# Routing stage with the residual add on VectorE, another order of instructions and another way into the experts; last pass with the hidden blocks transposed through memory and VectorE

## The reference

```python
x = x + tanh(g_xattn) * ssm(ctx, layernorm(x))          # the scan; its result is the "gated" addend
xn = layernorm(x)
scores = sigmoid(xn @ gate_w.T); sc = scores + gate_bias
# 4 groups of 8 experts: keep the 2 groups with the largest sum of their top two, then the top 4 experts
idx = top_k(where(group kept, sc, 0), 4); w = scores[idx] / sum(scores[idx]) * 2.0
# each expert takes its first 256 tokens in order, later ones are dropped
routed = sum_k w_k * (silu(xn @ w1[e]) * (xn @ w3[e])) @ w2[e]
shared = (silu(xn @ shared_gate) * (xn @ shared_up)) @ shared_down      # hidden width 1024
out = x + tanh(g_ffn) * (routed + shared)
```

## Time and profile before

| what | value |
|---|---|
| median of 3 runs | 4038.11 us (4036.43 to 4038.69) |
| the profiled execution, its own time | 4033.5 us |
| its span in the trace | 4031.7 us |
| busy: PE, DVE, ACT, POOL | 3681.9, 3111.3, 2114.9, 2008.3 us |
| routing stage / experts / last pass | about 1725 to 2386 / 2386 to 3479 / 3479 to 4032 us |

### The profile page before, as it was taken

The page is one execution under the profiler, slowest core; times in us unless marked ns, Lnnn a source line. Parts: engine busy times, 40 slices in busy tenths (PEclk is TensorE's granted clock), DMA queues, the critical chain, the costliest instruction groups (busy, mean ns, idle before and its releaser), DMA issues. The chain is left out here.

```text
span 4031.7 us, 58882 instructions
## 1 busy us (share of the span) xinstructions
PE 3681.9 (91%) x20528; PEld 3051.6 (76%) x20528; DVE 3111.3 (77%) x3712; ACT 2114.9 (52%) x2610; POOL 2008.3 (50%) x1201
## 2 busy tenths in 40 slices
PE   8898498888888888869999979999999999999999
PEld 3444388888878888758887868888888888788887
DVE  7899899999999999978888866666666666455555
ACT  3678699889989989821111134444444444200000
POOL 0233199999999999923333333333333333122222
PEclk9999599999999999979999989999999999999999
DMA  7677853653553553377766667777777777677543
GB/s 235 242 280 277 288 166 101 167 163 111 151 174 116 147 168 120 99 235 218 225 215 211 225 209 255 249 251 250 248 253 248 250 252 250 224 281 257 196 161 120
DMA packets 374393, 835.44 MB, mean 207 GB/s; under 512 B 96656, under 2 KB 155792, under 8 KB 364880
## 3 DMA queue, kind: packets, MB, share of 16 engines
q1 hardware_dynamic: 339264, 765.97, 56.3%
q0 software_dynamic: 34816, 67.24, 5.8%
q10 hardware_dynamic: 144, 0.00, 0.0%
HBM read 619.21 MB, written 245.27 MB: 214 GB/s over the span
## 5 line engine op out<-in xcount | busy, mean ns | idle before, releaser
L1125 POOL TENSOR_TENSOR h<-h,c 128x1024 f32<-128x1024 f32 x512 | 1206.4, 2417 | 24.4 <-DVE h L1108 21.5
L1108 DVE TENSOR_TENSOR_SCAN h<-da,dbu 128x1024 f32<-128x1024 f32 x512 | 1135.2, 2273 | 47.1 <-ACT dbu L1070 27.9
L1078 ACT ACTIVATE da<-dl,ad 128x1024 f32<-128x1024 f32 x512 | 584.2, 1141 | 100.3 <-DVE h L1108 88.9
L1157 PE MATMUL psy<-ident,h 128*128 128x128 f32 x4096 | 562.1, 281 | 81.6 <-POOL h L1125 60.6
L1903 POOL DMA_INDIRECT xg<-scratch_xn,ids x256 | 328.9, 1285 | 597.9 <-DVE xT_place L2190 520.1
L1070 ACT ACTIVATE dbu<-psb 128x512 f32<-128x512 f32 x1020 | 548.0, 589 | 30.7 <-PE psb L1147 27.9
L1157 PEld LDWEIGHTS psy<-ident,h 128*128 128x128 f32 x4096 | 444.9, 142 | 129.6 <-POOL h L1125 91.2
L2195 DVE TENSOR_TENSOR wsp<-arena,wsp 128x2048 fp32r<-128x2048 f32 x146 | 329.7, 2287 | 91.9 <-ACT wsp L2140 91.8
L1147 PE MATMUL psb<-m,du_taps 128*128 128x128 f32 x2048 | 294.6, 291 | 43.6 <-ACT dbu L1070 35.1
L1147 PEld LDWEIGHTS psb<-m,du_taps 128*128 128x128 f32 x2048 | 259.3, 193 | 79.5 <-ACT dbu L1070 73.0
L1451 POOL DMA_INDIRECT scratch_tab<-tok_s,si_s x128 | 132.1, 1032 | 358.8 <-DVE si_s L1819 327.4
(11 more groups left out here) (244 smaller groups left out, 8667.2 us busy)
## 6 DMA issues: line engine op xcount, KB each, us to landing
arena<-in_w SPq DMA_DIRECT2D x192, 1024.0 KB, 7.0
du_taps<-scratch_duT SPq DMA_DIRECT2D x496, 128.0 KB, 2.9
c<-scratch_c SPq DMA_DIRECT2D x64, 512.0 KB, 13.0
scratch_xT<-xT_s SPq DMA_DIRECT2D x32, 1024.0 KB
scratch_ob<-ob SPq DMA_DIRECT2D x64, 512.0 KB, 2.6
xT_place<-scratch_xT SPq DMA_DIRECT2D x32, 1024.0 KB, 4.9
scratch_duT<-duT SPq DMA_DIRECT2D x52, 512.0 KB, 4.0
xz<-in_x SPq DMA_DIRECT2D x32, 512.0 KB, 5.5
```

Of the source, the lines that this page charges most:

```text
L1078: act.activation(da[k % 2][:, :], dl[:, i % 2, :], ACT.Exp, scale=ad[:, i % 2, n:n + 1]).then_inc(s_da, 1)
L1108: dve.tensor_tensor_scan(h[:, k % HR, :], da[k % 2][:, :], dbu[:, (k // GN) % 2, k % GN, :], 0.0, ALU.mult, ALU.add).then_inc(s_scan, 1)
L1125: pool.tensor_tensor(h[:, k % HR, :], h[:, k % HR, :], c[:, n, :], ALU.mult).then_inc(s_hc, 1)
L1157: mm = pe.matmul(psy[:, t, :], h[:, k % HR, t * P:(t + 1) * P], ident[:], is_transpose=True, start=(n == 0 and t % 4 == 0), stop=(n == NST ...
```

## The change

In the **routing stage** the residual add goes from GpSimd to VectorE (in `norm`), the normalised tile is written by ScalarE (`normalise`, as scale * x + bias with bias = -mean * scale) and no longer by VectorE (`permuted` is gone), the Newton step has two instructions and no longer three, and VectorE's order is another: norm first, then queue, h_rest, x_blocks, choose, x_rest, multiply.

On the **way to the experts** the w2 matrix of expert 0 is loaded at the end of the routing stage, the rest of w3 is made after the first tile of rows (`first_up_rest`), w1 of expert 1 is loaded only after that, and VectorE multiplies expert 0's first hidden tile earlier.

In the **last pass** TensorE's `h_transpose` is gone. ScalarE stores the hidden tile to memory (`store_hidden`), waits for that, reads it back in four quarters (`load_hidden`), VectorE transposes 32x32 blocks (`h_blocks`), and head and rest are made from it. `finish` stands behind `h_rest`, and in it the read of `psO` comes first.

The core of the diff (renamings, semaphores and the like left out):

```diff
     for _ in range(NEWTON):
         st.then(dve.scalar_tensor_tensor(out=tmp[:, 1:2], in0=y, scalar=y, in1=tmp[:, 0:1], op0=ALU.mult, op1=ALU.mult))
-        st.then(dve.tensor_scalar(tmp[:, 1:2], tmp[:, 1:2], -0.5, 1.5, ALU.mult, ALU.add))
-        st.then(dve.tensor_tensor(y, y, tmp[:, 1:2], ALU.mult))
+        st.then(dve.scalar_tensor_tensor(out=y, in0=tmp[:, 1:2], scalar=1.5, in1=y, op0=ALU.add, op1=ALU.mult))
...
             if route:
                 first_ids()
+                for half in range(2):
+
+                    sp.wait_ge(s_wlo, 6 + half + 1)
+                    sp.dma_start(raw[:, 0, halves[half]].rearrange("p (k f) -> p k f", k=KF // 2),
+                                 io["w2"][0].rearrange("(h k p) f -> h p k f", h=2, p=P)[half]).then_inc(early["w2"][half], 16)
...
-                        if not (isinstance(t, int) and t >= TT - 3):
-                            add_x(j + 1 + par, 1 - par)
...
-                    if not route and not first:
-                        h_transpose(t - 1)
...
+            def normalise(t, j, par):
+
+                act.wait_ge(s_sc, t + 1)
+                after(act, s_xnst[par], j * 16)
+                act.activation(xn[:, par, :].rearrange("p (q j c) -> p j q c", q=NQ, c=QB),
+                               xt[:, par, :].rearrange("p (j q c) -> p j q c", q=NQ, c=QB), ACT.Identity, bias=rstd[:, 1:2],
+                               scale=rstd[:, 0:1]).then_inc(s_xn, 1)
...
+                    if not route and not first:
+                        load_hidden(t - 1)
                     if not first:
                         h_head(t - 1)
+                    if route and not first and not (isinstance(t, int) and t >= TT - 2):
+                        normalise(t + 2, j + 1, par)
 
                     act.wait_ge(s_g, t + 1)
-                    after(act, s_htr, t)
-                    act.activation(sg[:], psG[:], ACT.Silu).then_inc(s_sg, 1)
+                    if route:
+                        after(act, s_htr, t)
+                    act.activation(gated_hidden, gate_product, ACT.Silu).then_inc(s_sg, 1)
+                    if not route:
+                        store_hidden(t)
...
+            def store_hidden(t):
+
+                act.wait_ge(s_h, t + 1)
+                act.dma_start(dr["h"][t], sg[:]).then_inc(s_hst, 16)
+
+            def load_hidden(t):
+
+                act.wait_ge(s_hst, t * 16 + 16)
+                after(act, s_hlo, t)
+                for q in range(NQ):
+                    act.dma_start(hq[q * QB:(q + 1) * QB, :].rearrange("p (g c) -> p g c", g=NQ),
+                                  dr["h"][t][:, q * P:(q + 1) * P].rearrange("(g p) c -> p g c", g=NQ)).then_inc(s_hq, 16)
...
+            def h_blocks(t):
+
+                dve.wait_ge(s_hq, (t + 1) * 16 * NQ)
+                dve.transpose(hq[:], hq[:]).then_inc(s_htr, 1)
...
             def finish(t, j, par):
...
                 dve.wait_ge(s_acl[par], j * 32 + 32)
+                if not last:
+                    half()
...
-                dve.wait_ge(s_d, t + 1)
-                dve.scalar_tensor_tensor(out=x1t[:, par, :], in0=psO[:], scalar=gate[:, 0:1], in1=x1t[:, par, :],
-                                         op0=ALU.mult, op1=ALU.add).then_inc(s_half, 1)
+                if last:
+                    half()
...
                 after(dve, s_xn, t)
...
+                dve.tensor_tensor(xt[:, par, :], xt[:, par, :], xin[:, par, :], ALU.add).then_inc(s_add, 1)
...
-                    if route and not first:
-                        queue(t - 1, j - (par == 0), 1 - par)
                     if route and first:
                         norm(1, 0, 1)
                     elif route and not (isinstance(t, int) and t >= TT - 2):
                         norm(t + 2, j + 1, par)
+                    if route and not first:
+                        queue(t - 1, j - (par == 0), 1 - par)
+                    if not route and not first:
+                        h_blocks(t - 1)
+                    if not first:
+                        h_rest(t - 1)
                     if not route and not second:
                         finish(t - 2, j - 1, par)
-                    if not first:
-                        h_rest(t - 1)
+                    if route and not last and not first:
+                        x_blocks(t + 1, j + par, 1 - par)
                     if route:
                         choose(t)
-                    if route and not last and not first:
-                        x_blocks(t + 1, j + par, 1 - par)
...
-            load_matrix(0, 0, 2)
+            sp.wait_ge(early["up"], 2)
             load_matrix(1, 1, 0)
...
+                if t == 0:
+                    first_up_rest()
```

## The result

| | time, median of the runs | span of the profiled execution | granted clock |
|---|---|---|---|
| before | 4037.45 us (4036.43 to 4038.69, 4 runs) | 4031.7 | 0.974 |
| after | 4235.0 us (4227.74 to 4238.74, 4 runs) | 4231.4 | 0.949 |

The ratio is 1.0487, 95% interval 1.0469 to 1.0505: slower by 198 us. The forecast was slower by 29, the range ended at 4135, and the time lies outside it.

What follows compares the result with a forecast made beforehand. It took VectorE's list to bound most routing tiles and TensorE the last pass; -43 - 8 - 2 + 78 + 3 = +28 on 4033.5 gave 4061.5, or 4066 us on the median, range 4010 to 4135.

Steps and rivals of the forecast that it cites:

- Routing stage, -43 and -8: Routing stage: tiles fall from 19.26 to 17.6 us, saving 43 us over 26 tiles; the first three tiles save 8.
- The lock: Routing stage: VectorE's instruction with two SBUF inputs stands until GpSimd's residual add ends, 2.0 us a tile.
- VectorE's sum of 17.15: Routing stage: VectorE's predicted time per tile after the edits, 17.15 us, less than TensorE's 17.45.
- Way to the experts, -2: Between routing and experts: earlier w2 load clears DMA queues, less VectorE's added work; -2 us, between -4.5 and +2.
- Ring of the last pass: Last pass: VectorE's transposition waits for a store and load begun after its multiply; 19.4 us a turn, +78 us.
- The fixed part: Last pass: one turn without the store's time and the last quarter's landing, 12.5 us with overlap of neighbours.
- The 16.35 for TensorE's tile: Last pass: TensorE's 16.79 us tile without its 0.44 us transposition, 16.35 us if TensorE alone decided.
- S, 3.8: Last pass: time of the hidden tile's store to memory, taken as 3.8 us, the middle of 2.82 and 4.85.
- L, 3.1: Last pass: landing time of the last quarter of the hidden tile read back, taken as 3.1 us.
- Rival B: Last pass: quarters share engines with SyncE's 2 MB, the store with gathers; 21.85 us a turn, 4140 us, chance 0.15.
- The lower clock: Last pass: TensorE may run part of each tile at lower clock after waiting; up to 3 us of loss stays covered.
- Tail, +2: End of the last pass: the last down product starts some 11 us behind the last multiply, 9.0 before; +2 us.

Runs made afterwards that it cites:

- before_dve_add: Kernel before with only the routing stage's residual add moved from GpSimd to VectorE, SyncE's first stores ordered as in the changed kernel: 4013.7 us.
- big_pieces: Changed kernel with the hidden tile stored by four DMAs that lay out its blocks and loaded by one DMA of 2 KB rows: 4194.7 us.

## Why the prediction was wrong

By its own steps:

- **Routing stage, -43 and -8: right.** 17.53 us a tile against 17.6, and -51.9 from the first logits to the last (602.24 and 550.36) against -51. TensorE is the bound as said. The lock exists and is worth what was said where VectorE is the bound (before_dve_add, -0.74 a tile). But VectorE's sum of 17.15 was too high: with the lock and without the add's 1.22 the tile still took only 17.66. By that VectorE alone would need at most 17.66 - 2.5 + 1.2 = 16.4. Some of the other edits gave more than I counted; which one was not tried. It cost nothing here, because TensorE covers it.
- **Way to the experts, -2: inside its range,** 0 there (-51.1 in all up to the first rest), and -4.1 from there to the last pass, which no term had; its cause was not tried.
- **Ring of the last pass: right as a mechanism.** The fixed part was 12.5; the tile shown has 0.84 + 2.19 + 9.95 = 12.98, by the prediction's count of L 12.4. It is what bounds: with its sums moved away or its transfers shortened, the time fell as the ring says, and under 16.32 TensorE took over. The 16.35 for TensorE's tile is confirmed too.
- **S, 3.8: too high,** 2.9. The store is issued 2.3 us before SyncE's first load.
- **L, 3.1: this is the step that failed.** It measured 11.4 early and 7.3 late. The mean turn is (767.87 - 22.96) / 30 = 24.83 instead of 19.4 (L some 6.4 more, S 0.9 less), which is 163 of the 174 us by which the last pass was missed; the other 11 are the first tile, 22.96 for 11.3 before, where I had put 1. I took L from the median landing of quarters in the routing stage, "nearer to the row of the same shape", and bounded it from above with the 4.5 of a load of SyncE. But how long a DMA takes to land is set here by what is in flight beside it, and by how many packets each of them has. I had written down that SyncE's 2 MB "start just before them" and that gathers start at the same moment, and did not divide: 2 MB at the 400 GB/s of the stretches above are 5 us, gathers of 2.1 MB 5 more, and with 576 packets of their own the quarters wait for nearly all of both. Rival B, the upper end, had the sharing in its words and the wrong price for it.
- **The lower clock: covered, as said.** The prediction let up to 3 us of it disappear in TensorE's idle time. TensorE waits 8.4 us in the tile shown and idles 6.3 in the mean turn, and in that tile VectorE waits for no product, so nothing in the time is put down to the lower clock.
- **Tail, +2: right,** +1.9.

For four quarters alone the trace has 1.77 us of issues and 1.5 behind them, 3.3 from the first issue; beside 4 MB it took 13.6. The Trainium skill, "DMA: Bandwidth & Descriptors", section "Anatomy of one DMA", fits a transfer that GpSimd issues with 2.0 us plus its bytes at 436 GB/s; the prediction used that for transfers that ScalarE issues. For the four quarters an estimate by it is 2.6, and the trace is near it where they are alone, and nowhere else.

The queues are served packet by packet: 241, 236 and 236 packets in the 6 us shown. The Trainium skill, "DMA: Bandwidth & Descriptors", section "Queues, rings and completion order", has each engine take turns between the queues that have work, a packet at a time. The trace agrees, as far as its own count of packets goes. What stays open is why the first packet of the quarters moves 0.95 us after the first issue when they are alone and some 3.7 us after it in a busy early tile. What is shown besides is that each of the two other streams costs the quarters about its bytes over 400 GB/s.

## What to carry to other kernels

A round trip through memory on the path of a tile costs its turns in the DMA queues. Count the packets, its own and those of the other queues: where its own are as many as theirs, it lands behind nearly all of their bytes, so add these up, divide by what the engines move when full, and add that to the landing. A transfer of fewer packets may get through sooner, as the load of big_pieces did, if the other half of the trip does not pay for it, as its stores did. Before closing such a ring, look at what stands between the two ends of it in the engine's list: here 7.9 us of sums did, and moving them ahead of the wait, which also put SyncE's loads behind the quarters, was worth 234 of the 253 us lost (767.87 - 533.62). Holding the other transfers back helps while their data have time to spare, and closes a new ring as soon as they have not. And two edits should be timed apart: one gained 59 us and hid under the other, which even at its best can only bring a tile from 16.79 to 16.32.

## What was not expected of the hardware

- Quarters of 512 B pieces landed 1.5 us behind the last issue alone, 6.8 beside 2.1 MB of gathers, 11.4 with 2 MB of another queue as well. Gathers whose rows are dropped (576 packets, 0.01 MB) cost them nothing: 1.6 us.
- The engines gave three queues 241, 236 and 236 packets in 6 us, which were 1.36, 0.90 and 0.11 MB.
- Sixteen small DMAs issued one after the other took 0.65 to 0.70 us each in the mean of a run's early or late tiles; four took 0.44 each when alone, 0.59 in the mean of the changed kernel's early tiles.
- VectorE's stand beside GpSimd's add is not bound to an instruction with two SBUF inputs: a cast with one input stood for 2.7 us. The Trainium skill, "SBUF — State Buffer", section "SBUF: two separate sides", names VectorE's two-port mode as another case of the lock. The cast would fit that, but no run here shows in which mode it ran.
- TensorE's granted clock fell from 1.00 to 0.50 (1.2 GHz) while it waited, in each tile of the last pass up to the thirtieth; the down products' matmuls took 0.49 us in the mean over the pass, where they take 0.39 at 1.00.
